# Attention and expert kernel: maxima pairs issued in a row, three PSUM banks used in turn, another order of SP's transfers

## What is computed

```python
x = x + tanh(g_xattn) * xattn(layernorm(x), ctx)      # 32 blocks, 8 heads of 16, 512 positions
x = x + tanh(g_ffn) * ffn(layernorm(x))               # router, top 2 of 8 experts, shared expert

# xattn, per block and head
q, k, v = proj(x, Wq, bq), proj(ctx, Wk, bk), proj(ctx, Wv, bv)
attn = softmax(q @ k.T / sqrt(16))                    # 512 x 512
out = attn @ v
```

## Time and profile before

| what | us |
|---|---|
| device time, median of 3 runs | 1480.17 |
| lowest and highest | 1476.13, 1481.53 |
| device time of the profiled execution | 1477.53 |
| its span | 1475.7 |
| TensorE busy (share of the span) | 1391.0 (94%) |
| VectorE, ScalarE, GpSimd busy | 991.7, 909.4, 868.9 |
| reductions of the maxima (VectorE, 512 of them) | 620.8 |
| exponentials (ScalarE, 1024 of them) | 587.0 |

### The profile page before, as it was taken

The page is one execution under the profiler, slowest core; times in us unless marked ns, Lnnn a source line. Parts: engine busy times, 40 slices in busy tenths (PEclk is TensorE's granted clock), DMA queues, the critical chain, the costliest instruction groups (busy, mean ns, idle before and its releaser), DMA issues.

```text
span 1475.7 us, 24574 instructions
## 1 busy us (share of the span) xinstructions
PE 1391.0 (94%) x7290; PEld 679.8 (46%) x7290; DVE 991.7 (67%) x1661; ACT 909.4 (62%) x1720; POOL 868.9 (59%) x1278
## 2 busy tenths in 40 slices
PE   3899999999999999999999999989999999999997
PEld 1222333322322232323322332258788788888886
DVE  5788888888788887888888887846764333333332
ACT  2488788887777777787778777743333433333332
POOL 7436676766777667776776774455211555555553
PEclk9999999999999999999999999999999999999999
DMA  5657666665666566666666755356653798886565
GB/s 159 166 147 219 178 181 211 185 181 166 202 176 179 155 198 182 175 167 198 188 181 165 206 164 149 105 162 157 155 175 98 165 215 205 195 199 109 108 114 79
DMA packets 161308, 247.90 MB, mean 168 GB/s; under 512 B 33605, under 2 KB 58828, under 8 KB 161182
## 3 DMA queue, kind: packets, MB, share of 16 engines
q1 hardware_dynamic: 142926, 208.96, 49.3%
q0 software_dynamic: 18256, 37.38, 13.7%
HBM read 141.85 MB, written 103.88 MB: 167 GB/s over the span
## 4 chain that ended last, share of the span: by engine, by line
PE 41%; DMA 22%; SPq 13%; issue 11%; POOL 7%; ACT 3%; DVE 2%; POOLq 1%; ACTq 0%
PE m_banks L1409 18%; PE bank L1337 7%; DMA arena<-pv_d 7%; SPq L468 7%; PE bank L1366 6%; DMA parts_q<-arena 5%; DMA rden_d<-arena 4%; PE m_banks L1315 3%; DMA arena<-m_rows 3%; DMA out<-xs,ids 2%; POOL xs L778 2%; PE bank L1296 2%; SPq L454 2%; PE bank L1342 1%; ACT arena L1163 1%
## 5 line engine op out<-in xcount | busy, mean ns | idle before, releaser
L892 DVE TENSOR_REDUCE row_max<-m_banks 128x2 f32<-128x1024 f32 x512 | 620.8, 1221 | 135.7 <-PE m_banks L1315 128.5
L1163 ACT ACTIVATE arena<-bank 128x512 f32<-128x512 f32 x1024 | 587.0, 600 | 179.6 <-PE bank L1337 164.5
L1337 PE MATMUL bank<-arena 112*128 112x512 bf16 x1024 | 400.0, 393 | 40.6 <-ACT arena L1163 19.9
L1366 PE MATMUL bank<-arena 128*32 128x512 f32 x2048 | 278.0, 615 | 0.0
L1337 PEld LDWEIGHTS bank<-arena 112*128 112x128 bf16 x1024 | 101.0, 99 | 369.6 <-ACT arena L1163 212.2
L1315 PE MATMUL m_banks<-arena 48*128 48x512 bf16 x1024 | 205.4, 399 | 11.5 <-DMA arena<-parts_q 6.1
L790 POOL DMA_INDIRECT out<-xs,ids x71 | 112.5, 1585 | 173.2 <-ACT xs L1237 139.5
L1409 PE MATMUL m_banks<-w_ring,h_hi 128*128 x568 | 183.0, 403 | 0.0
L1226 ACT ACTIVATE arena<-m_banks 128x256 f32<-128x256 f32 x103 | 39.5, 384 | 190.0 <-PE m_banks L1409 187.3
L684 POOL TENSOR_TENSOR arena<-arena 128x512 f32<-128x512 f32 x32 | 40.7, 1272 | 166.1 <-DMA arena<-pv_d 162.7
L1315 PEld LDWEIGHTS m_banks<-arena 48*128 48x128 bf16 x1024 | 49.2, 93 | 172.1 <-issue 97.5
(11 more groups left out here) (176 smaller groups left out, 2029.6 us busy)
## 6 DMA issues: line engine op xcount, KB each, us to landing
pv_d<-arena SPq DMA_DIRECT2D x32, 512.0 KB, 6.6
w_ring<-split_d SPq DMA_DIRECT2D x60, 256.0 KB
parts_k<-arena SPq DMA_DIRECT2D x96, 128.0 KB
parts_q<-arena SPq DMA_DIRECT2D x96, 128.0 KB
arena<-parts_k SPq DMA_DIRECT2D x64, 192.0 KB
arena<-parts_q SPq DMA_DIRECT2D x64, 192.0 KB
arena<-in_w SPq DMA_DIRECT2D x36, 256.0 KB, 5.9
arena<-in_ctx SPq DMA_DIRECT2D x32, 256.0 KB
```

The costliest lines, as they stand in the source:

```text
L892: nc.vector.reduce_max(pair, m_ps[(STEPS * b + u) // 2 % M_PAIRS], AX_X).then_inc(s_mx, 1)
L1163: nc.scalar.activation(probs[group % 3][:, j, :], e_ps[n % E_BANKS], ACT.Exp, scale=float(DH) ** -0.5).then_inc(s_exp, 1)
L1337: nc.tensor.matmul(e_ps[n % E_BANKS], k_stack[b % 3][0:SHIFTED, h, kt * P:(kt + 1) * P], q_stack[b % 3][0:SHIFTED, h, :], start=True, stop ...
L1366: last = nc.tensor.matmul(pv_ps[2 * DH * j:2 * DH * (j + 1), :], v_ones[b % 3][:, kt, GROUP * g + j, :], probs[pair % 3][:, j, :], start=( ...
```

## The change

1. TensorE issues a group as score, score, maxima pair, maxima pair, (extra work), score, score, (values). Before, the extra work stood between the second and the third score as well.
2. The scores no longer have two banks and the extra work a third of its own: banks 0, 1 and 7 (`turning`) are taken in turn by whatever comes next (`take_bank`), and each taker waits for the reader of what was in the bank it gets. `bank_of` tells the readers where to look. A turn takes 32 banks for scores and 7 (in every fourth turn 8) for the rest. The expert phase keeps bank 7.
3. On SP the row transfers of half 1 go ahead of the values' store, the queries' reads go behind the reciprocals' store, and the keys' writes go to the end of the turn.
4. VectorE's reciprocal moves from step 19 to step 16.

```diff
-RECIP_AT = 19
+RECIP_AT = 16
...
-        E_BANKS, M_PAIRS = 2, 2
-        e_ps = banks[0:E_BANKS]
+        M_PAIRS = 2
+        turning = [banks[0], banks[1], banks[7]]
...
-        pv_ps, misc_ps = banks[6:8]
+        pv_ps = banks[6]
+        bank_of = {}
...
-                if is_b(i - 1):
-                    store_values(i - 1)
-                if is_b(i):
-                    row(i, 1)
+                if is_b(i):
+                    row(i, 1)
+                if is_b(i - 1):
+                    store_values(i - 1)
...
+            def take_bank(user, reader, count, at=None):
+                if at is None:
+                    at = taken[0] % len(turning)
+                    taken[0] += 1
+                if last_reader[at]:
+                    pe.wait_ge(*last_reader[at])
+                last_reader[at] = (reader, count)
+                bank_of[user] = turning[at]
+                return turning[at]
...
-                take_misc(s_mr, 2 * b + half + 1)
-                nc.tensor.transpose(misc_ps[0:n, 0:P], row_max[b % 2][:, n * half:n * (half + 1)],
+                out = take_bank(("maxima", b, half), s_mr, 2 * b + half + 1)
+                nc.tensor.transpose(out[0:n, 0:P], row_max[b % 2][:, n * half:n * (half + 1)],
...
-                if n >= E_BANKS:
-                    pe.wait_ge(s_exp, n - E_BANKS + 1)
-                nc.tensor.matmul(e_ps[n % E_BANKS], k_stack[b % 3][0:SHIFTED, h, kt * P:(kt + 1) * P],
+                out = take_bank(("scores", b, s), s_exp, n + 1)
+                nc.tensor.matmul(out, k_stack[b % 3][0:SHIFTED, h, kt * P:(kt + 1) * P],
```

More of the change, by code:

```diff
@@ L550, in _ @@
                     store_reciprocals(i - 1)
+                if is_b(i + 2):
+                    read(i + 2, 1)
                 if is_b(i + 1):
@@ L565, in _ @@
                     load_staged(i + 3)
+                if is_b(i + 3):
+                    for part in (HI, MID, LO):
+                        write(i + 3, 0, part)
                 for r in SHARED_ROWS.get(i, ()):
@@ L876, in take_logits @@
                     dve.wait_ge(s_map0, 3 * DMA)
-                nc.vector.tensor_copy(logits[:, b * EXPERTS:(b + 1) * EXPERTS], misc_ps[:, 0:EXPERTS]
+                nc.vector.tensor_copy(logits[:, b * EXPERTS:(b + 1) * EXPERTS], bank_of["logits", b][:, 0:EXPERTS]
                                       ).then_inc(s_lc, 1)
@@ L895, in maxima_rows @@
                 n = GROUP * KT
+                turned = bank_of["maxima", b, half][0:n, 0:P]
                 dve.wait_ge(s_mt, 2 * b + half + 1)
@@ L899, in maxima_rows @@
                 return chain(
-                    lambda: nc.vector.tensor_scalar(m_rows[half][:, 0, :], misc_ps[0:n, 0:P], -1.0, None, ALU.mult),
-                    lambda: nc.vector.scalar_tensor_tensor(m_rows[half][:, 1, :], misc_ps[0:n, 0:P], -1.0,
+                    lambda: nc.vector.tensor_scalar(m_rows[half][:, 0, :], turned, -1.0, None, ALU.mult),
+                    lambda: nc.vector.scalar_tensor_tensor(m_rows[half][:, 1, :], turned, -1.0,
                                                            m_rows[half][:, 0, :], ALU.mult, ALU.subtract
@@ L1145, in evacuate @@
                         act_e.wait_ge(s_wr[n], 3 * DMA * b)
-                    nc.scalar.activation(proj[n], misc_ps, ACT.Identity, bias=bias[:, n:n + 1]).then_inc(s_evac, 1)
+                    nc.scalar.activation(proj[n], bank_of["projection", b, n], ACT.Identity, bias=bias[:, n:n + 1]).then_inc(s_evac, 1)
                     return
@@ L1150, in evacuate @@
                 nc.scalar.copy(v_ones[b % 3][:, :, :, 0:DH],
-                               misc_ps.rearrange("p (t h d) -> p t h d", t=KT, h=HEADS)).then_inc(s_evac, 1)
+                               bank_of["projection", b, n].rearrange("p (t h d) -> p t h d", t=KT, h=HEADS)).then_inc(s_evac, 1)
             def high_part(b, n):
@@ L1162, in exponential @@
                     act_e.wait_ge(s_pv, group - 2)
-                nc.scalar.activation(probs[group % 3][:, j, :], e_ps[n % E_BANKS], ACT.Exp,
+                nc.scalar.activation(probs[group % 3][:, j, :], bank_of["scores", b, s], ACT.Exp,
                                      scale=float(DH) ** -0.5).then_inc(s_exp, 1)
@@ L1176, in take_turned @@
                     act_e.wait_ge(s_hts, DMA * b)
-                nc.scalar.copy(tok_t.rearrange("p c n -> p (c n)"), misc_ps).then_inc(s_hf, 1)
+                nc.scalar.copy(tok_t.rearrange("p c n -> p (c n)"), bank_of["tokens", b]).then_inc(s_hf, 1)
             def staged_high(k):
```

389 lines of the change are left out of this document (191 added, 198 removed).

## The result

| | before | after |
|---|---|---|
| device time, median of 4 runs each on one chip, us | 1478.15 | 1559.45 |
| lowest and highest | 1475.21, 1481.53 | 1556.87, 1563.14 |
| ratio, 95% interval | | 1.0551 [1.0516, 1.0586] |
| span of the profiled execution | 1475.7 | 1558.4 |
| TensorE, VectorE busy | 1391.0, 991.7 | 1379.7, 979.1 |

What follows compares the result with a forecast made beforehand. TensorE was taken as the bound, at 29.03 us a turn. A turn of 30.1 adds 29 us over 28 turns, the last turn returns 3: 1477.5 becomes 1503; the clock's +28 - 9 makes 1522 us, range 1482 to 1565.

Steps and rivals of the forecast that it cites:

- Like after like: On TensorE, a matmul following one of its own form takes a step of 0.22 us; a bare group falls to 2.62.
- Rival (5): Matmuls following their like are no cheaper: +1 us a turn, adding 28 us; chance 0.14 together with the spread slow clock.
- E6: Score matmul in a turn's second group; waits for VectorE's maxima rows, a new 1.7 us, starting at 5.5.
- E0: First score matmul of a turn, from which times in the turn are counted; the next one was put at 30.1 us.
- The reciprocal and T in g4: Fifth group: reciprocal waits about 1.7 us for denominators, starts at 17.5; maxima transposition behind it at 18.1 instead of 17.1.
- rival (3): The denominators' wait is hidden if the reciprocal starts by 16.5: turn 29.1, time 1477 us; chance 0.10.
- E22: Score matmul in a turn's sixth group; waits for VectorE's maxima rows until 21.5, a new 2.2 us.
- The sum of the waits: Whole attention phase: turn 30.1 us, +1.05 a turn over 28 turns, less 3, giving 1503 us with the clock as before.
- the last turn: End of the attention phase: it has no maxima, so TensorE gives back about 3 us.
- The clock: One slow stretch a turn after the new waits costs 1.0 us, +28; less 9 already carried by the kernel before.
- Rival (2): Slow clock spreads to two stretches a turn, +64 us, 1560 us; chance 0.14 together with like matmuls being no cheaper.
- SP's order: Half 1's row transfers land early, removing 14.5 us of row waits; values' store 1.2 us later; moved reads cost little.

Runs made afterwards that it cites:

- the array kept busy: The changed kernel plus 7 and 9 unread score matmuls a turn in TensorE's two waits for the maxima rows; 1504.6 us, ratio 1.0205 to the kernel before.
- own-bank kernel: The changed kernel with only the sharing undone: scores take two banks in turn, everything else the third; 1483.3 us, ratio 1.0048 to the kernel before.

## Why the prediction came out

1559.45 lies in the range, near its upper end, and on the forecast side, 37 us above the likeliest time. The mechanism, two waits for the rows in a turn and a slow clock behind them, is the one that the runs show; about 25 of the 37 us are the clock's term and about 11 that of the waits.

- **Like after like.** Held. Two scores take 0.60 where one takes 0.38 or 0.39, so the step is 0.22, and the bare group from 619.11 to 621.82 takes 2.71 (2.62 computed). Rival (5) falls.
- **E6.** The wait was put at 1.7 and is 1.63; E6 starts 5.60 after E0 (5.5 computed).
- **The reciprocal and T in g4.** Missed. SP issued rows, store and denominators' load of that turn at

```profile
624.67 1.21 SPq L529 DMA_DIRECT2D arena<-m_rows  x2
625.99 1.24 SPq L479 DMA_DIRECT2D pv_d<-arena  x1
...
632.60 0.64 SPq L485 DMA_DIRECT2D arena<-pv_d  x1
```

and the reciprocal started at 635.49. Store to load is 6.6 (7.0 taken) and load to reciprocal 2.9 (3.85 taken), so it started at 16.4 and not 17.5. VectorE waited 14.0 us in all instead of 1.7 a turn, T hardly at all (2.9 us in the whole phase, 1.0 a turn computed). The condition of rival (3), a reciprocal by 16.5, was met in this turn: T stands 17.33 after E0. Its time, 1477, was not, and not for the clock alone: even with the array kept busy the turn was 29.87 and not 29.1.

- **E22.** Put at 2.2; it is 2.08 in this turn and 3.32 in the next. VectorE there:

```profile
668.39 1.23 DVE L1122 TENSOR_REDUCE row_max<-m_banks 128x2 f32<-128x1024 f32 x1 [0.85 <-PE m_banks L856]
669.53 0.61 DVE L1169 TENSOR_TENSOR route<-route 128x32 f32<-128x32 f32 x1
670.17 0.28 DVE L1131 TENSOR_SCALAR m_rows<-bank 16x128 bf16<-16x128 f32 x1
670.49 0.99 DVE L1170 TENSOR_TENSOR route<-route 128x32 f32<-128x32 f32 x1
671.51 0.28 DVE L1132 SCALAR_TENSOR_TENSOR m_rows<-bank,m_rows 16x128 bf16<-16x128 f32 x1
```

Two routing steps stand between the reduction and the second row operation: 3.40 from the reduction's start to the end, the long case of the earlier trace rows. Operation L1170 took 0.99 us here and 0.19 in the turn before; why, no run shows. Of 124.0 us, 52.5 are E6's and the other 71.5 E22's, 2.4 each.

- **The sum of the waits.** 1503, with a turn of 30.1. The run with the array kept busy, which has the waits' length without their idling, gave 29.87 and by its ratio 1508. That looks like a hit and is partly luck. The 1503 still has in it the slow clock of the kernel before, some 12 us by the estimate above, and the run has almost none of it, so the waits cost some 11 us more than computed: 81 - 44 = 37 instead of 26. Part of this is the last turn. It was to give 3 us back, but VectorE's casts of the shared expert's weights stood ahead of its rows, and its E6 waited longest of all:

```profile
1034.75 0.61 PE L877 MATMUL bank<-arena 112*128 112x512 bf16 x2 [3.55 <-DVE m_rows L1132]
```

The time that T did not lose went partly into E22's longer waits.

- **The clock.** The right mechanism and the wrong size; this is the term that missed by most. The stretch was put at a third of 10.24 us (3.41 measured) and at one per turn, but there were 38 such lengths and not 28. And each us of them cost 0.43 net of all that later waits took up, where the prediction's 1.0 us for a stretch is 0.29. Computed +28 - 9 = 19; by the estimate above it was 56 - 12 = 44. Rival (2), 1560, has the time, but with two stretches a turn; there were 35 in 31 turns, so that its figure fits is luck.
- **SP's order.** Half right. The rows' transfers of half 1 did land early. That the moved reads "cost the next rows little" held only because the two new waits gave SP's rows 10 us until they were needed (640.04 to 649.96); alone, the order made the waits for the rows' transfer 25.0 us instead of 14.5.

## What to carry to other kernels

When buffers are pooled in a rotation, every user inherits the slowest reader in it: before sharing a bank, look up on the reader's engine what stands ahead of the reading instruction, and move the reader first (here 7% for two instructions moved). Price a wait on TensorE as the wait plus the clock that it takes down behind it: here an estimated 44 of the 81 us that the change cost. A step on a serial DMA queue is worth what it hides as well as what it delays, so try such an order as a whole and in the kernel it is meant for.

## What the runs showed of the hardware

- Two waits of 1.63 and 1.2 to 3.3 us in a turn of 32 us, with TensorE otherwise busy nearly without a break, brought the 1.2 GHz level about once a turn (35 stretches in 31 turns); the own-bank kernel, with 34.0 us in 65 waits of at most 0.6 us for ScalarE and 31 longer ones of 25.7 us in all, had 5.
- Matmuls that nobody reads, placed in the two waits, held the granted clock at 1.00 in the turns and made the kernel 3.3% faster.
- A row transfer of 4 KB issued directly behind six reads of 64 to 192 KB was waited for until 8.4 us after its issue. Whether the reads or other traffic held it up stays open: undoing the reads' move changed SP's whole stream.
